# Two-part scores and a later cast in the attention stage of a fused GNN kernel

## The chip, the core and the metric
The kernel runs on one core of a Trainium2 chip. The time is the device time of one execution in microseconds. The kernel before takes 1899.82 us, the median of 3 runs (1897.61 to 1903.91).

## What is computed
The input is x (3125 nodes, 768 features, float32) and 50000 edges (src, dst) sorted by dst. Two layers with a layer norm, a relu and a residual each follow one another: a two-step graph convolution, and a graph attention with 12 heads of 64 features. The change touches only the attention:

```python
hh = h.reshape(n, H, D)
ft = einsum('nhd,ed->nhe', hh, W_fc)
a1 = einsum('nhd,hd->nh', ft, attn_l)
a2 = einsum('nhd,hd->nh', ft, attn_r)
e = leaky_relu(a1[src] + a2[dst], 0.2)
m = segment_max(e, dst)
ee = exp(e - m[dst])
denom = segment_sum(ee, dst)
agg = segment_sum((ee / denom[dst])[:, :, None] * ft[src], dst)
res = einsum('nhd,ed->nhe', hh, W_res)
x = x + relu((res + agg).reshape(n, H * D))
```

## The kernel before, in words
Destination nodes are cut into 25 tiles of 128 rows (the last has 53). A tile's edges are worked on in quads; with these inputs every tile has one quad, so there are 25 visits. A quad has four units, one for each 32 destination rows, of up to 512 edges each (4 chunks of 128), and one shared chunk for what is left over: 17 chunks. Each chunk is one indirect DMA of 128 rows from the table in HBM; a row holds, per head, 64 features and a one (780 numbers), and 12 score terms a1 behind them. The last visit has two units (9 chunks).

The engines run side by side, each with its own program, and meet at semaphores. `ring` has two halves, so a quad's rows are fetched while the quad before is computed.

- GpSimd (POOL, `fetch`, L1243): for quad q it waits until its slots (row numbers) are in, then asks for units 0, 1, 2, the shared chunk and unit 3 in this order. Before each unit it waits for `used[s]`: TensorE must have finished the products of quad q-2 out of the same part of the ring.
- VectorE (DVE): `carry`, then the maximum of the scores with their sloped copy (L1613), two scans for the segment maximum (L1616, L1619), the difference (L1621), the division for the tile before (L1567 to L1573), then it waits for the exponentials (`w_made`) and scales the rows of units 0, 1 and 2 by them (L1650, `scaled[s]`). Behind unit 2 it waits for all rows of the next quad to have landed and copies their terms (L1561, L1562, `take_terms`, `terms_in`). Then the shared chunk (L1657), the finish of tile j-2 (L1579) and the one-hots of quad q+2 (L1555).
- ScalarE (ACT, `follow`): casts the quad's one-hots to float32 (L1344, `cast_hot`, `hot_cast`), the exponentials for DVE (L1368, `w_made`) and for itself (L1372), a copy of the next quad's transposed one-hots (L1330), the tile's a2 (L1325), unit 3's rows scaled in 48 pieces (L1388), the sloped copy of the next scores (L1336, needs `z_sum` of TensorE), and `lay` for the tile before (L1354, 16 pieces).
- TensorE (PE, `visit`): transposes the differences (L1471, `t_made`) and the next one-hots (L1442), the residual product of tile j-2 (L1419), clears the accumulators (L1483), the products of units 0, 1 and 2 (L1492, each behind `scaled[s]`, all behind `hot_cast`), the next quad's scores (`scores(q + 1)`), the shared chunk's products (L1507) and unit 3's (L1492). `scores` has two kinds of terms, added in the same PSUM window: four matmul groups out of the one-hots, a2 and a constant (L1454 to L1457), and five that add the fetched terms (L1461), behind `terms_in`; the last sets `z_sum`.
- SyncE (SP): per visit one store of a finished tile (384 KB, L1277), one load of the turned activations (384 KB, L1268), the slots of quad q+2 (L1261) and four small loads (L1265). The two 384 KB transfers begin with the third visit.

By parity of q, TensorE's product code exists twice, and a branch picks one (`by_parity`).

Of the kernel before, what the change touches and what calls it, by code (L numbers as in the profile page):

```python
# [69 lines left out]
def gnn_kernel(nc, x, src, dst, w1t, b1, w2t, b2, wfc, wfct, attn_lt, attn_rt, wrest, out):  # L70
# [21 lines left out]
    with ctx:  # L92
# [984 lines left out]
        with ExitStack() as st:  # L1077
# [84 lines left out]
            def window(c0, n):  # L1162
                return ps_s[0:UH, W0 + c0:W0 + c0 + n]
# [7 lines left out]
            def is_last(j):  # L1171
                return isinstance(j, int) and j == NT - 1

            def units_of(j):
                return LU if isinstance(j, int) and j == NT - 1 else US


            def early_of(j):
                return min(3, units_of(j) - 1)
# [4 lines left out]
            def by_parity(eng, which, body):  # L1184
                with eng.If(which < 1):
                    body(0)
                with eng.Else():
                    body(1)
# [20 lines left out]
            def quad_bounds(eng):  # L1209
                return (eng.value_load(qptr[0:1, NT - 1:NT], min_val=1, max_val=QMAX), eng.value_load(qptr[0:1, NT:NT + 1], min_val=1, max_val=QMAX))  # L1210
# [9 lines left out]
            def tiles(eng, step):  # L1220
                for j in range(2):
                    step(j)
                with eng.Fori(2, NT - 1) as j:
                    step(j)
                step(NT - 1)

            def has_before(j, back=1):
                return not isinstance(j, int) or j >= back
            with nc.Block() as block:
# [87 lines left out]
                @block.scalar  # L1317
                def _(eng):
                    bounds = quad_bounds(eng)
                    eng.wait_ge(g_const, 2)  # L1320

                    def a2_of(j):
                        for s in range(US):
                            r = slice(s * UD, (s + 1) * UD)
                            last = eng.activation(a2_blk[r, s * H:(s + 1) * H], a2[r, ds(j, 1), :].rearrange("p a h -> p (a h)"), ACT.Copy)  # L1325
                        last.then_inc(a2_made, 1)

                    def turn_hot(q):
                        eng.wait_ge(hot_tr, q + 1)
                        eng.activation(hot_t[:, :, :].rearrange("p c e -> p (c e)"), ps_ht, ACT.Copy).then_inc(hot_tc, 1)  # L1330


                    def sloped(q):
                        eng.wait_ge(z_sum, q + 1)
                        eng.wait_ge(c_chain, q + 1)
                        eng.activation(top[:, 1:1 + WIN], window(0, WIN), ACT.Copy, scale=SLOPE).then_inc(z_low, 1)  # L1336

                    def cast_hot(q, j):
                        eng.wait_ge(hot_made, q + 1)
                        eng.wait_ge(used[units_of(j) - 1], q + 2)  # L1340
                        if units_of(j) < US:
                            eng.wait_ge(used[US - 1], bounds[0] + 2)
                        par = eng.snap(q % 2)
                        eng.activation(hot_f[:, :, :].rearrange("p c e -> p (c e)"), hot[:, ds(par, 1), :, :].rearrange("p a c e -> p (a c e)"), ACT.Copy).then_inc(hot_cast, 1)  # L1344


                    def lay(j):
                        eng.wait_ge(o_made, j + 1)
                        eng.sem_inc(passed, 1)
                        eng.wait_ge(o_fin, j + 1)  # L1350
                        for g in range(US):
                            for s in range(US):
                                c0 = g // 2 * 512 + g % 2 * GN
                                last = eng.activation(ps_n[s * UD:(s + 1) * UD, c0:c0 + GN], o[g * UD:(g + 1) * UD, s, :], ACT.Copy)  # L1354
                        last.then_inc(o_laid, 1)

                    def step(j):
                        mine = units_of(j) - 1

                        def follow(q, nth, left):  # L1360
                            cast_hot(q, j)
                            with eng.If(nth < 1):
                                eng.sem_inc(r_exp, 1)
                            with eng.Else():
                                eng.wait_ge(r_diff, q + 1)
                                eng.activation(ex[:, 1:2], ex[:, 0:1], ACT.Exp).then_inc(r_exp, 1)
                            eng.wait_ge(t_made, q + 1)
                            eng.activation(given_w, ps_e, ACT.Exp).then_inc(w_made, 1)  # L1368
                            if is_last(j):
                                eng.sem_inc(own_made, 1)  # L1370
                            else:
                                eng.activation(weight[:, :, :], ps_e[:, 0:CPU, mine * H:(mine + 1) * H], ACT.Exp).then_inc(own_made, 1)  # L1372
                            turn_hot(q + 1)
                            with eng.If(left < 2):
                                a2_of(j + 1)
                            with eng.Else():
                                eng.sem_inc(a2_made, 1)
                            if is_last(j):
                                with eng.If(nth < 1):
                                    lay(j - 1)  # L1380
                                sloped(q + 1)
                                return
                            eng.wait_ge(own_made, q + 1)
                            rows = ring[:, ds(eng.snap(eng.snap(q % 2) * RB + mine * CPU * FROW), CPU * FROW)]
                            for c in range(CPU):
                                for h in range(H):
                                    head = rows[:, c * FROW + h * FH:c * FROW + (h + 1) * FH]
                                    last = eng.activation(head, head, ACT.Copy, scale=weight[:, c, h:h + 1])  # L1388
                            last.then_inc(scaled[mine], 1)
                            sloped(q + 1)  # L1390
                            if has_before(j):
                                with eng.If(nth < 1):
                                    lay(j - 1)
                        tile_quads(eng, j, follow)
                    turn_hot(0)
                    a2_of(0)
                    sloped(0)
                    tiles(eng, step)

                @block.tensor  # L1400
                def _(eng):
# [42 lines left out]

                    def scores(q):
                        eng.wait_ge(hot_tc, q + 1)
                        eng.wait_ge(a2_made, q + 1)
                        if not isinstance(q, int):  # L1450
                            eng.wait_ge(w_made, q)
                            eng.wait_ge(own_made, q)
                        eng.sem_inc(passed, 1)
                        eng.matmul(window(0, P), a2_blk[:, :], hot_t[:, 0, :], start=True, stop=True, skip_group_check=True)  # L1454
                        eng.matmul(window(CPU * P, P), far[:, :].to_broadcast([P, UH]), ident[:, :], start=True, stop=True, skip_group_check=True)
                        eng.matmul(window(CPU * P, P), far_of[:, :], hot_t[:, CPU, :], start=False, stop=True, skip_group_check=True)
                        eng.matmul(window(P, CPU * P), a2_blk[:, :], hot_t[:, 1:UC, :].rearrange("p c e -> p (c e)"), start=False, stop=True, skip_group_check=True)  # L1457
                        eng.wait_ge(terms_in, q + 1)
                        eng.sem_inc(passed, 1)
                        for c in range(UC):  # L1460
                            last = eng.matmul(window(c * P, P), terms[:, c, :], ident[:, :], start=False, stop=True, skip_group_check=True)  # L1461
                        last.then_inc(z_sum, 1)

                    def step(j):
                        nu = units_of(j)

                        def visit(q, nth, left):
# [26 lines left out]
                                last.then_inc(used[s], 1)  # L1494

                            def first_products(b):
                                for s in range(early_of(j)):
                                    unit(b, s)

                            def other_products(b):  # L1500
# [10 lines left out]
                            eng.wait_ge(hot_cast, q + 1)  # L1511
                            eng.sem_inc(passed, 1)
                            by_parity(eng, eng.snap(q % 2), first_products)
                            scores(q + 1)
                            by_parity(eng, eng.snap(q % 2), other_products)
                        tile_quads(eng, j, visit)
                    turn_hot(0, 0)
                    scores(0)
                    tiles(eng, step)
                    natural(NT - 2)  # L1520

# [188 lines left out]
```

## Time and profile before

| what | value |
|---|---|
| median of 3 runs | 1899.82 us |
| profiled execution, its own time | 1901.22 us |
| its span | 1899.5 us |
| PE, DVE, ACT, POOL busy | 1327.0, 1123.7, 716.8, 1234.5 us |
| attention stage | from about 1300 us to the end |
| granted TensorE clock, mean | 0.881 |

The page shows shares over the whole span. The attention is the last third: from 1400 to 1800 us DVE is busy 84 to 86%, ACT 89 to 90%, POOL 75 to 76%, PE 64 to 70%, and the DMA engines 96 to 97%. None of these shares alone says what sets the pace; the stretch has to be read visit by visit, which recurs about every 22.3 us.

### The profile page before, as it was taken

Reading aid. Unit: us, or ns where it says so; the run is one execution under the profiler, and the core shown is the slowest. Engines: PE = TensorE matmul, PEld = TensorE weight load, DVE = VectorE, ACT = ScalarE, POOL = GpSimd, SP = SyncE. Lnnn points to the kernel's source line nnn. Section 1 sums busy time; section 2 is a strip of 40 time slices with the busy share of each in tenths; the row PEclk is TensorE's granted clock in tenths of the full one; section 3 lists DMA queues with packets and bytes.
Section 4 is the critical chain, followed back from the end, with each engine's and each line's share of the span. In section 5 each row is a group of like instructions: output and inputs, shape, how many; then the busy total and the mean of one; then the engine's idle time right before and its main releaser. Section 6 shows DMA issues by size and latency. Waiting matters only on the chain. (4 is left out here: it accounts for less than half of the span.)

```text
span 1899.5 us, 43588 instructions
## 1 busy us (share of the span) xinstructions
PE 1327.0 (70%) x13579; PEld 879.2 (46%) x13580; DVE 1123.7 (59%) x2027; ACT 716.8 (38%) x2184; POOL 1234.5 (65%) x1297
## 2 busy tenths in 40 slices
PE   6426877787877847777777777793566676677665
PEld 6314444444544524444444444492344544444453
DVE  6623454444544525545555555562788888888887
ACT  6600111111111100001000010171688998989885
POOL 3137777777777457777777777204777777777760
PEclk9977898989999978899999899997788878888887
DMA  6589999999999679999999999388999999999992
GB/s 219 208 210 361 331 328 336 333 332 331 335 334 330 230 239 334 330 324 329 323 333 334 330 326 331 140 322 291 314 335 347 348 352 347 345 347 343 357 320 69
DMA packets 139991, 585.22 MB, mean 308 GB/s; under 512 B 30615, under 2 KB 32751, under 8 KB 139945
## 3 DMA queue, kind: packets, MB, share of 16 engines
q0 software_dynamic: 100272, 497.49, 74.3%
q1 hardware_dynamic: 32563, 67.72, 10.1%
q10 hardware_dynamic: 7110, 19.43, 2.9%
q8 instruction: 25, 0.41, 0.1%
q14 instruction: 21, 0.17, 0.0%
HBM read 534.42 MB, written 50.12 MB: 308 GB/s over the span
## 5 line engine op out<-in xcount | busy, mean ns | idle before, releaser
L667 POOL DMA_INDIRECT ring_c<-table,slot_c x834 | 797.0, 956 | 313.6 <-issue 293.9
L1243 POOL DMA_INDIRECT ring<-table,slot x417 | 413.3, 991 | 141.5 <-issue 115.9
L711 ACT ACTIVATE slot_c<-units 128x8 int32 (+1 forms) x104 | 21.7, 210 | 857.9 <-DMA ring_c<-table,slot_c 812.0
L1388 ACT ACTIVATE ring<-ring,weight x1152 | 279.0, 335 | 0.6
L833 DVE TENSOR_TENSOR hots<-iota,units 128x256 f32<-128x256 bf16 x102 | 43.5, 428 | 391.3 <-PE ps_sum0a L779 123.0
L1650 DVE TENSOR_TENSOR ring<-ring,ps_w 128x3120 f32 x72 | 242.7, 3398 | 16.8 <-ACT ps_w L1368 16.5
L1492 PE MATMUL ps_acc<-ring,hot_f 128*32 128x195 f32 x3136 | 179.1, 376 | 86.0 <-DVE ring L1650 84.1
L808 PE MATMUL ps_ya<-weights,sum_ta 128*128 128x512 f32 (+1 forms) x576 | 190.9, 488 | 0.0
L808 PE MATMUL ps_yb<-weights,sum_tb 128*128 128x512 f32 (+1 forms) x576 | 189.7, 486 | 0.0
L1492 PEld LDWEIGHTS ps_acc<-ring,hot_f 128*32 128x32 f32 x3136 | 105.1, 124 | 148.1 <-DVE ring L1650 109.3
L808 PEld LDWEIGHTS ps_ya<-weights,sum_ta 128*128 128x128 f32 x576 | 110.2, 191 | 77.3 <-issue 69.6
L808 PEld LDWEIGHTS ps_yb<-weights,sum_tb 128*128 128x128 f32 x576 | 109.5, 190 | 76.4 <-issue 68.9
L779 PE MATMUL ps_sum0a<-ring_c,hots 128*32 128x192 f32 x1600 | 86.4, 368 | 78.5 <-DMA ring_c<-table,slot_c 78.5
L779 PE MATMUL ps_sum0b<-ring_c,hots 128*32 128x192 f32 x1600 | 84.9, 361 | 70.0 <-DMA ring_c<-table,slot_c 70.0
L779 PE MATMUL ps_sum1b<-ring_c,hots 128*32 128x192 f32 x1536 | 85.5, 373 | 64.2 <-DMA ring_c<-table,slot_c 64.2
L779 PE MATMUL ps_sum1a<-ring_c,hots 128*32 128x192 f32 x1536 | 85.7, 373 | 62.4 <-DMA ring_c<-table,slot_c 62.4
L1354 ACT ACTIVATE ps_n<-o_g 32x192 f32<-32x192 f32 x384 | 124.6, 324 | 7.7 <-DVE nodes L1579 3.6
L779 PEld LDWEIGHTS ps_sum0a<-ring_c,hots 128*32 128x32 f32 x1600 | 57.9, 121 | 104.8 <-issue 75.0
L779 PEld LDWEIGHTS ps_sum0b<-ring_c,hots 128*32 128x32 f32 x1600 | 57.5, 118 | 95.5 <-issue 79.9
L779 PEld LDWEIGHTS ps_sum1b<-ring_c,hots 128*32 128x32 f32 x1536 | 57.0, 122 | 90.5 <-issue 77.3
L779 PEld LDWEIGHTS ps_sum1a<-ring_c,hots 128*32 128x32 f32 x1536 | 56.9, 122 | 88.7 <-issue 79.2
L854 DVE TENSOR_TENSOR ps_sum0a<-ps_sum0a,naturala 32x192 f32<-32x192 f32 x200 | 73.3, 367 | 8.3 <-ACT naturala L739 5.7
(294 smaller groups left out, 1940.2 us busy)
## 6 DMA issues: line engine op xcount, KB each, us to landing
ring_c<-table,slot_c POOLq DMA_INDIRECT x834, 5.4
table<-ft SPq DMA_DIRECT2D x25, 396.0 KB, 2.8
table<-nodes SPq DMA_DIRECT2D x25, 384.0 KB, 3.3
table<-nodes ACTq DMA_DIRECT2D x25, 384.0 KB, 5.3
turned_table<-h_t SPq DMA_DIRECT2D x25, 384.0 KB, 3.0
nodes<-in_x ACTq DMA_DIRECT2D x24, 384.0 KB
turned_g<-turned_table SPq DMA_DIRECT2D x24, 384.0 KB, 6.5
out_x<-nodes SPq DMA_DIRECT2D x24, 384.0 KB
```

What stands on the lines that cost most here:

```text
L667: eng.indirect_dma_start(out=ring[:, t * QH + k, :], out_offset=None, in_=table, in_offset=bass.IndirectOffsetOnAxis(ap=slot[t][:, k:k + 1 ...
L711: eng.activation(slot[t][:, :], units[:, ds(q, 1), t * QH:(t + 1) * QH + t].rearrange("p a c -> p (a c)"), ACT.Copy).then_inc(slot_ready[t ...
L779: last = eng.matmul(block_of(par, s, g), hot, rows[:, g * GB:(g + 1) * GB], start=start, stop=True, skip_group_check=True)
L808: last = eng.matmul(product(jj)[:, c0:c0 + n], turned(jj)[:, k, :], w[:, k, c0:c0 + n], start=(k == 0), stop=(k == KB - 1))
L833: eng.tensor_tensor(hots[k][:, :, :].rearrange("p (s c) d -> p s c d", c=CPU), iota0[:, :].unsqueeze(1).unsqueeze(2).to_broadcast([P, 2, C ...
L854: last = eng.tensor_tensor(block_, block_, natural[s * UD:(s + 1) * UD, g * GB:(g + 1) * GB], ALU.add)
L1243: eng.indirect_dma_start(out=ring[:, b * RB + at * FROW:b * RB + (at + 1) * FROW], out_offset=None, in_=table3, in_offset=bass.IndirectOff ...
L1354: last = eng.activation(ps_n[s * UD:(s + 1) * UD, c0:c0 + GN], o[g * UD:(g + 1) * UD, s, :], ACT.Copy)
L1388: last = eng.activation(head, head, ACT.Copy, scale=weight[:, c, h:h + 1])
L1492: last = eng.matmul(acc_of(s, g), hot_f[:, c, s * UD:(s + 1) * UD], ring[:, x0 + g * GW:x0 + (g + 1) * GW], start=False, stop=True, skip_g ...
L1650: eng.tensor_tensor(mine, mine, given_w[:, 0:CPU, s * H:(s + 1) * H].unsqueeze(3).to_broadcast([P, CPU, H, FH]), ALU.mult).then_inc(scaled ...
```

## The change
In `follow` on ScalarE the cast of the one-hots is moved from the head of the visit to behind the two exponentials. On TensorE `scores` is split. Its first part (`scores_of_hots`, L1454 to L1457 with the waits for the one-hots, a2 and the exponentials of the quad) is issued behind unit 1's products, its second part (`scores_of_terms`, with the wait for `terms_in`) behind unit 2's. Unit 2's products get a parity branch of their own (`next_products`). The last tile has `early_of` 1 and no such branch. No arithmetic instruction is added or removed; the branch and one more increment of `passed` are.

```diff
 def follow(q, nth, left):
-    cast_hot(q, j)
     with eng.If(nth < 1):
         eng.sem_inc(r_exp, 1)
...
         eng.activation(weight[:, :, :], ps_e[:, 0:CPU, mine * H:(mine + 1) * H], ACT.Exp).then_inc(own_made, 1)
+    cast_hot(q, j)
     turn_hot(q + 1)
...
-def scores(q):
+def scores_of_hots(q):
     eng.wait_ge(hot_tc, q + 1)
     eng.wait_ge(a2_made, q + 1)
...
     eng.matmul(window(P, CPU * P), a2_blk[:, :], hot_t[:, 1:UC, :].rearrange("p c e -> p (c e)"), start=False, stop=True, skip_group_check=True)
+
+def scores_of_terms(q):
     eng.wait_ge(terms_in, q + 1)
     eng.sem_inc(passed, 1)
     for c in range(UC):
...
 def first_products(b):
-    for s in range(early_of(j)):
+    for s in range(min(2, early_of(j))):
+        unit(b, s)
+
+def next_products(b):
+    for s in range(2, early_of(j)):
         unit(b, s)
...
 by_parity(eng, eng.snap(q % 2), first_products)
-scores(q + 1)
+scores_of_hots(q + 1)
+if early_of(j) > 2:
+    by_parity(eng, eng.snap(q % 2), next_products)
+scores_of_terms(q + 1)
 by_parity(eng, eng.snap(q % 2), other_products)
```

## Rows read from the trace of the kernel before

**Rows 1.** The chain that ended last over the whole span, by engine.
```profile
issue 9%; POOL 5%; DVE 5%; ACT 4%; PE 3%; DMA 2%; DVEq 1%; ACTq 1%; SPq 0%; POOLq 0%
```

**Rows 2.** Busy time by windows: stretch, length, engines, PEclk, DMA share, GB/s.
```profile
1322.00:1343.60 21.60, 7.13 (x62) 4.89 (x66) 12.62 (x11) 10.50 (x35) 16.16 (x17) 0.50 0.93 319
1389.00:1835.00 446.00, 305.52 (x4040) 214.94 (x4040) 379.51 (x341) 398.03 (x1461) 338.02 (x341) 0.83 0.97 348
```

**Rows 3.** Timeline of one visit: start, length, engine, line, operation, idle before.
```profile
1564.81 6.71 DVE L1650 TENSOR_TENSOR ring<-ring,ps_w 128x3120 f32 x2
1568.26 1.75 PE L1492 MATMUL ps_acc<-ring,hot_f 128*32 128x195 f32 x32 [0.60 <-DVE ring L1650]
1571.58 1.53 PE L1492 MATMUL ps_acc<-ring,hot_f 128*32 128x195 f32 x32 [1.57 <-DVE ring L1650]
1572.25 0.22 DVE L1562 COPY terms<-ring 128x48 f32 x1
1573.72 1.02 PE L1457 MATMUL ps_s<-hot_t,a_blk 128*48 128x512 f32 x2
1574.58 1.26 PE L1461 MATMUL ps_s<-ident,terms 128*48 128x128 f32 x10
1575.88 0.70 ACT L1336 ACTIVATE top_g<-ps_s 48x640 f32<-48x640 f32 x1 [1.64 <-PE ps_s L1461]
1576.47 5.37 ACT L1354 ACTIVATE ps_n<-o_g 32x192 f32<-32x192 f32 x16
1580.73 0.82 DVE L1621 TENSOR_TENSOR score<-ps_s,top_g 48x640 f32<-48x640 f32 x1
1581.69 0.48 PE L1471 MATMUL ps_s<-ident,score 48*128 48x48 f32 x5 [3.07 <-DVE score L1621]
1582.27 0.74 ACT L1344 ACTIVATE hot_f<-hot 128x640 f32 x1 [0.43 <-issue]
1583.03 0.35 ACT L1368 ACTIVATE ps_w<-ps_s 128x240 f32<-128x240 f32 x1
1587.05 6.71 DVE L1650 TENSOR_TENSOR ring<-ring,ps_w 128x3120 f32 x2
```

**Rows 4.** Gathers on POOL, timeline; where a fetch starts, and a long one.
```profile
1367.36 0.94 POOL L1243 DMA_INDIRECT ring<-table,slot  x1 [2.58 <-PE ps_acc L1492]
1435.00 0.95 POOL L1243 DMA_INDIRECT ring<-table,slot  x1 [1.79 <-PE ps_acc L1492]
1457.00 0.95 POOL L1243 DMA_INDIRECT ring<-table,slot  x1 [0.30 <-issue]
1523.95 0.94 POOL L1243 DMA_INDIRECT ring<-table,slot  x1 [0.52 <-issue]
1568.51 0.94 POOL L1243 DMA_INDIRECT ring<-table,slot  x1 [0.52 <-issue]
1579.81 1.64 POOL L1243 DMA_INDIRECT ring<-table,slot  x1 [0.30 <-issue]
1590.48 0.95 POOL L1243 DMA_INDIRECT ring<-table,slot  x1 [0.30 <-issue]
1601.73 2.19 POOL L1243 DMA_INDIRECT ring<-table,slot  x1 [0.30 <-issue]
1835.38 0.95 POOL L1243 DMA_INDIRECT ring<-table,slot  x1 [0.30 <-issue]
```

**Rows 5.** The first visit's scores, timeline.
```profile
1350.75 1.06 PE L1457 MATMUL ps_s<-hot_t,a_blk 128*48 128x512 f32 x2 [2.06 <-issue]
```

**Rows 6.** The end of the stage, timeline.
```profile
1839.33 0.26 DVE L1561 COPY terms<-ring 128x192 f32 x1 [0.72 <-DMA ring<-table,slot]
1842.96 0.70 ACT L1336 ACTIVATE top_g<-ps_s 48x640 f32<-48x640 f32 x1 [1.64 <-PE ps_s L1461]
1860.89 1.53 PE L1492 MATMUL ps_acc<-ring,hot_f 128*32 128x195 f32 x32 [1.17 <-DVE ring L1650]
1865.19 0.70 ACT L1336 ACTIVATE top_g<-ps_s 48x640 f32<-48x640 f32 x1 [1.63 <-PE ps_s L1461]
```

More of the change, by code:

```diff
@@ L1517, in _ @@
                     turn_hot(0, 0)
-                    scores(0)
+                    scores_of_hots(0)
+                    scores_of_terms(0)
                     tiles(eng, step)
```

## The prediction, made before the changed kernel had run

> **What bounds the kernel now.** I read the whole-span chain of waits first, then windows over the attention stage, then one visit as a timeline, then every gather. The chain is mixed: no engine has more than a few per cent [rows 1]. So shares don't decide, and I look for loops. From 1389 to 1835 us twenty visits pass at 22.3 us each, with ACT busy 398 of 446 us, DVE 380, POOL 338, and the DMA engines at a share of 0.97 with 348 GB/s [rows 2].
>
> Loop A goes through DVE, PE and ACT, once a visit [rows 3]. DVE's third unit ends at 1564.81 + 6.71 = 1571.52. PE then does unit 2 (1571.58 + 1.53 = 1573.11), the one-hot groups (until 1573.72 + 1.02 = 1574.74) and the terms (until 1575.84). ACT's sloped copy ends at 1576.58. DVE's scans end with the difference at 1580.73 + 0.82 = 1581.55. PE's transposes end at 1582.17. ACT first does the cast (1582.27 to 1583.01), and only then the exponentials (1583.03 to 1583.38). DVE scales three units, until 1587.05 + 6.71 = 1593.76. From 1571.52 to 1593.76 are 22.24 us, and nothing in the loop waits for anything outside it. The terms were ready at 1572.47, 2.1 us before PE used them: the landing of rows is not on this loop now.
>
> Loop B is POOL: 17 gathers, each 0.945 + 0.303 us from start to start, make 21.22 us. One or two gathers of a fetch take longer (1579.81 lasts 1.64 us, 1601.73 lasts 2.19, [rows 4]); this comes about 5 us behind the two 384 KB transfers of a visit. Before these transfers exist the fetch from 1322 took 21.3 us at 319 GB/s [rows 2]. I take the excess for back-pressure of the DMA. It is 0.69 to 0.88 us in the fetches that began with a small wait (0.69 in the one gather of 1.64). Third, POOL waits for unit 0's products at a fetch's start: the gap is about 0.52 us in place of 0.30 in 13 fetches between 1411 and 1814 us, as at 1523.95 and 1568.51, once 1.79 (1435.00) and once 2.58 (1367.36) [rows 4]. 21.22 + 0.76 + 0.22 = 22.2: A and B are tied, with A ahead by the small wait.
>
> **The change part by part.** The cast. PE's transposes end at 1582.17 and ACT's `lay` at 1576.47 + 5.37 = 1581.84; the cast starts 0.43 us behind it. Without it the exponentials can start at about 1582.35 instead of 1583.03: 0.65 us less in loop A (bounds 0.5 and 0.74, the cast's own length). ACT's work from there on (copy of one-hots, a2, unit 3's rows) starts no later than now, as the total ahead of it is the same. `hot_cast` comes later by the two exponentials, at about 1583.7, but the first product that needs it starts when unit 0 is scaled, at 1587. Its waits for `used` and `hot_made` move behind the exponentials, which so lose them; both are met long before.
>
> The split. PE is idle from unit 1's end (1568.26 + 1.75 = 1570.01) to 1571.58. The one-hot groups take 1574.74 - 1573.11 = 1.6 us there, 0.3 us of control around them: unit 2 begins 0.1 to 0.5 us late. Then the terms follow unit 2 at once. From DVE's third unit to `z_sum` there are 4.32 us now; then 0.3 + 1.55 + 0.3 + 1.25 = 3.4. Gain 0.9 us (bounds: 0.3, if each of three new control steps costs 0.5; and 1.7, if all is hidden). All waits of the first part (transposed one-hots, a2, both exponentials) are met 7 us before. Behind it on PE's queue stand unit 2's products and POOL's unit 2 gathers, which need them only some 5 us later.
>
> Loop A falls to 22.24 - 0.65 - 0.9 = 20.7 us, so loop B sets the pace. What the time gains is what POOL stops waiting, and the ends of the stage, where POOL doesn't bind.
>
> Start: the wait of 2.58 - 0.30 = 2.28 us before the fetch at 1367.36 [rows 4]. It hangs on the scores of the second quad, which in the first visit ended late, behind a pause of 2.06 us inside the one-hot groups that nothing in the profile explains [rows 5]. The split brings these scores forward by 3.4 us if the pause falls in PE's idle time, by 1.1 if it moves to the terms; the cast was hidden there. I take 1.7 of 2.28 (bounds 0.5 and 2.28).
>
> The wait at 1435.00: 1.79 - 0.30 = 1.49 us, goes whole, since loop A is 1.5 us shorter in each of the visits before (bounds 1.0 and 1.49).
>
> The small waits: 13 of about 0.225, 2.9 us. Here the question is what the long gathers do. Five fetches began without a wait and without a large one just before; their excess was 0.97 to 1.25, as in the one that starts at 1590.48 and holds the 2.19 us gather [rows 4], against 0.75 behind a small wait: as if DMA took back what was given. But the fetch at 1435.00, without a wait behind it, had 0.75 as well. I take half, 1.5 us (bounds: the mean excess of the 20 fetches from 1389 us on is 0.84; at 1.25 in each 8.3 us are lost and 2.9 won back, 5.4 lost; at 0.75 in each 1.7 come on top of the 2.9, 4.6 won).
>
> End [rows 6]: the last full quad's rows are there at 1839.3 and its terms at 1839.8. PE finishes their scores at about 1842.93 now, and could at 1839.8 + 0.3 + 1.25 = 1841.4: 1.5. One exponential, 0.6. In the visit behind it DVE sets the pace: its third unit ends at 1860.84, the scores at 1865.15; 4.3 to 3.6 gives 0.7. The last visit's exponential comes 0.6 earlier by the cast. From there everything follows in the old order (the last visit has no part 2 branch). Sum 3.4 (bounds 2.2 and 4.0).
>
> Sum: 1.7 + 1.5 + 1.5 + 3.4 = 8.1 us. The profiled execution took 1901.2 (span 1899.5), so 1893.1 by its measure; it lies 1.4 above the median, which gives 1891.7 for the median, as 1892. Bounds: 0.5 + 1.0 - 5.4 + 2.2 = -1.7 and 2.3 + 1.5 + 4.6 + 4.0 = 12.4.
>
> On the DMA the rows show 348 GB/s as a mean at a share of 0.97 over twenty visits [rows 2], 7.75 MB a visit. The Trainium skill (DMA: Bandwidth & Descriptors, section Where 436 GB/s comes from) names about 358 GB/s as what HBM gives one core, and about 435 as what the ports carry. By the first a visit can't be under 21.6 us, which is below loop B; but so near to it that little can be won, and it speaks for the first rival. The same page says that single-core measurements reach 425.
>
> **The rivals.** First: DMA binds, and each removed wait comes back as a longer gather (fetches at 22.25 us, as the three between 1457.00 and 1523.95, the last followed by a small wait [rows 4]: 66.95 - 0.22 = 66.7). For it: DMA share 0.97, excess of 1.0 without waits. Against: the fetch at 1568.51 took 1590.48 - 1568.51 = 21.97. The 21 fetches from 1367.36 to 1835.38 took 468.0, at 22.25 they take 467.3; with 1.7 and 3.4 at the ends the gain is 5.8 us: 1894.
>
> Second: all waits go and the excess stays at 0.75. For it: 13 of 20 fetches show it. 2.3 + 1.5 + 4.6 + 4.0 = 12.4: 1887.
>
> Third: the split does nothing (the terms wait behind a late unit 2), and only the cast counts. Loop A then is 21.6 us, which still frees POOL: 0.2 + 1.5 + 1.5 + 3 x 0.6 = 5: 1895.
>
> Fourth, slower: PE pays a pause like the 2.06 us [rows 5] in each visit, at the new branch or behind it, on the way to the terms. Loop A is then 20.7 + 2.06 = 22.8 us and binds again: 20 x (22.8 - 22.3) = 10, and about 1 at the ends: 1911. It decides from a pause of 1.6 us on. For it: the pause exists, and the loop's code gets one more jump. Against: behind both present branches PE's steady visits show gaps of only 0.3 us. The Trainium skill (Runtime: NRT & Kernel Launch, section Instruction fetch mechanics) says that a taken branch out of the loaded window stalls for a fetch; the present branches over longer code show no such stall in steady visits.
>
> **How the numbers follow.** A measurement of this kernel can tell about 0.3%, 5.7 us, from no change: faster is below 1894.1, slower above 1905.5. The forecast has 0.50, of which a good four fifths lie below 1894.1; DMA binds 0.20, somewhat under half of it below; all waits go 0.13; only the cast 0.10, a third of it below; slower 0.07. Faster: 0.42 + 0.09 + 0.13 + 0.04 = 0.68; same 0.25; slower 0.07. The range from 1886 to 1899 takes in the first three rivals and most of the bounds.
>
> **What would show it.** The exponential starts within 0.3 us of the transposes' end. One-hot groups stand between units 1 and 2, and the terms start within 0.5 us of unit 2 or of the terms' copy. DVE's wait for landed rows grows from 0.6 to 1.1 to about 2 us a visit. POOL's gaps at a fetch's start are all 0.30 us; the excess of the long gathers is 0.75 to 1.0 a fetch (1.0 and more: first rival). Fetches follow every 22.0 to 22.2 us. The prediction is wrong if the visits get shorter than 21.9 us (the excess was no back-pressure), if PE pauses by over 1.6 us ahead of the terms, or if the stage's end keeps its length.

## The result, and the profile after

The changed kernel takes 1890.35 us (median of 8 runs, 1886.72 to 1893.94), the kernel before 1903.43 beside it on the same chip (8 runs, 1897.61 to 1904.87). The ratio is 0.994, with a 95% interval from 0.9926 to 0.9955: 8.6 to 14.1 us less, 11.4 by the ratio itself (the two medians lie 13.1 apart). The profiled execution took 1886.80 us with a span of 1885.0.

Where it went, by the starts of fetches (a fetch is the 17 gathers of one quad) in the two traces. The columns are the start of the stage's first gather, the time from it to the start of the 4th fetch, the 21 fetches from there, and the rest, in us:

```
kernel   first gather  to 4th fetch  21 fetches   to the end  stage total
before      1300.76        66.60       468.02       64.12        598.7
after       1295.28        65.45       462.65       61.62        589.7
```

"Stage total" is the span less the first gather's start. Of the 14.5 us between the two spans 5.5 lie ahead of the stage, where the code is the same; over nine profiled executions on this kind of chip, the kernels of the experiments below among them, the first gather starts anywhere from 1295.2 to 1301.3. So 9.0 us are the change's: 1.15 at the start, 5.37 in the middle, 2.50 at the end. Each kernel has one trace; how much the stage itself varies between executions is not known.

The middle of the stage, one window of the kernel after, with the columns of [rows 2]:

```profile
1389.00:1823.00 434.00, 292.21 (x3962) 208.76 (x3958) 374.43 (x336) 391.96 (x1433) 332.04 (x335) 0.85 0.97 352
```

One visit of the kernel after as a timeline, as in [rows 3]:

```profile
1555.60 6.71 DVE L1660 TENSOR_TENSOR ring<-ring,ps_w 128x3120 f32 x2
1561.20 1.02 PE L1457 MATMUL ps_s<-hot_t,a_blk 128*48 128x512 f32 x2
1562.23 0.25 DVE L1571 COPY terms<-ring 128x192 f32 x1
1562.37 1.53 PE L1494 MATMUL ps_acc<-ring,hot_f 128*32 128x195 f32 x32
1563.82 1.29 PE L1463 MATMUL ps_s<-ident,terms 128*48 128x128 f32 x10
1565.71 0.69 ACT L1336 ACTIVATE top_g<-ps_s 48x640 f32<-48x640 f32 x1
1571.51 0.48 PE L1473 MATMUL ps_s<-ident,score 48*128 48x48 f32 x5 [3.61 <-DVE score L1631]
1572.31 0.35 ACT L1367 ACTIVATE ps_w<-ps_s 128x240 f32<-128x240 f32 x1 [0.65 <-PE ps_s L1473]
1572.80 0.74 ACT L1344 ACTIVATE hot_f<-hot 128x640 f32 x1
1576.33 6.71 DVE L1660 TENSOR_TENSOR ring<-ring,ps_w 128x3120 f32 x2
1584.61 0.49 DVE L1571 COPY terms<-ring 128x192 f32 x1 [1.57 <-DMA ring<-table,slot]
1585.33 1.26 PE L1463 MATMUL ps_s<-ident,terms 128*48 128x128 f32 x10 [0.72 <-DVE terms L1572]
1588.11 0.70 ACT L1336 ACTIVATE top_g<-ps_s 48x640 f32<-48x640 f32 x1 [1.57 <-DVEq L1617]
```

The one-hots' groups stand ahead of unit 2, and the terms follow it at once. The exponentials start 0.32 us behind the transposes' end (1571.99), the cast behind them. DVE's third unit ended at 1555.60 + 6.71 = 1562.31 and ends again at 1576.33 + 6.71 = 1583.04: loop A is 20.73 us in this visit, where it was 22.24. The last three rows show what is late next: DVE waits 1.57 us for landed rows, and then ACT's sloped copy waits 1.57 us for DVE.

The waits of the middle (1380 to 1830 us) by who waited for what (us in total, times, longest). DVEq is DVE's sequencer:

```profile
DVE terms L1571 <- DMA ring<-table,slot: 26.8, 20, 1.8
ACT top_g L1336 <- DVEq L1617: 22.9, 18, 1.7
POOL ring L1243 <- PE ps_acc L1494: 6.7, 22, 0.3
```

And the fetches' first gathers on POOL, with the end of the stage's last full quads:

```profile
1360.73 0.94 POOL L1243 DMA_INDIRECT ring<-table,slot  x1 [1.32 <-PE ps_acc L1494]
1382.36 0.95 POOL L1243 DMA_INDIRECT ring<-table,slot  x1 [0.30 <-issue]
1823.38 0.95 POOL L1243 DMA_INDIRECT ring<-table,slot  x1 [0.30 <-issue]
1827.18 0.26 DVE L1571 COPY terms<-ring 128x192 f32 x1 [1.10 <-DMA ring<-table,slot]
1830.59 0.70 ACT L1336 ACTIVATE top_g<-ps_s 48x640 f32<-48x640 f32 x1 [1.01 <-DVEq L1617]
1837.20 0.35 ACT L1367 ACTIVATE ps_w<-ps_s 128x240 f32<-128x240 f32 x1 [0.65 <-PE ps_s L1473]
1857.66 0.35 ACT L1367 ACTIVATE ps_w<-ps_s 128x240 f32<-128x240 f32 x1 [0.38 <-PE ps_s L1473]
```

The 2.58 and 1.79 of [rows 4] are 1.32 and 0.30 now, and the small waits are 0.30 to 0.33 but for one of 0.48: 21 fetches take 462.65 us, 22.03 each.

### The profile page after: what moved, and what is told of

Its sections match the earlier page's. It is cut to its first block and busy times, and to the rows that moved or that the text cites. A ratio compares the mean times of both kernels' runs of the same rounds, so it can differ in the third digit from the quotient of the medians.

```text
span 1885.0 us, 43624 instructions
## 1 busy us (share of the span) xinstructions
PE 1328.8 (70%) x13579; PEld 879.1 (47%) x13580; DVE 1124.0 (60%) x2027; ACT 716.7 (38%) x2184; POOL 1230.6 (65%) x1297
## 5 line engine op out<-in xcount | busy, mean ns | idle before, releaser
L1494 PE MATMUL ps_acc<-ring,hot_f 128*32 128x195 f32 x3136 | 163.4, 352 | 50.9 <-DVE ring L1660 44.6
L1494 PEld LDWEIGHTS ps_acc<-ring,hot_f 128*32 128x32 f32 x3136 | 99.9, 117 | 114.5 <-DVE ring L1660 80.8
L779 PE MATMUL ps_sum1a<-ring_c,hots 128*32 128x192 f32 x1536 | 81.9, 364 | 57.7 <-DMA ring_c<-table,slot_c 57.6
L1473 PE MATMUL ps_s<-ident,score 48*128 48x48 f32 x125 | 16.7, 282 | 109.9 <-DVE score L1631 109.9
```

The costliest lines, as they stand in the source:

```text
L779: last = eng.matmul(block_of(par, s, g), hot, rows[:, g * GB:(g + 1) * GB], start=start, stop=True, skip_group_check=True)
L1494: last = eng.matmul(acc_of(s, g), hot_f[:, c, s * UD:(s + 1) * UD], ring[:, x0 + g * GW:x0 + (g + 1) * GW], start=False, stop=True, skip_g ...
```

## The experiments

### The parts one by one, and another order on SP

"Cast only" is the part of the change in ACT's list, "split only" that in PE's. "Early load" is the kernel after with SP's two large transfers in the other order:

```diff
-                            store(j - 2)
+                            eng.wait_ge(o_nat, j - 1)
+                            eng.sem_inc(passed, 1)
                             load_turned(j - 1)
+                            store(j - 2)
```

They ran first on another chip, beside the change itself.

> The changed kernel once more, beside the parts of it. My theory (the pace passed from the loop through DVE, PE and ACT to POOL's gathers): ratio 0.994 to 0.996, fetches every 22.0 to 22.2 us, sum of the attention stage from the first gather to the end 9 us shorter than before (589.7 against 598.7 us). The 5.5 us by which the first gather came earlier in the first profile of the changed kernel (1295.3 against 1300.8 us) are spread between executions and not the change: here the first gather may lie anywhere from 1294 to 1302. If the change also shortened the part ahead of the stage (by where its code lies), the first gather is again at 1295 to 1296.

> Only the cast is moved; the scores stay in one part behind unit 2. Theory: the loop through DVE, PE and ACT falls from 22.24 to about 21.6 us, already under POOL's pace of 22.0 to 22.2, so most of the gain in the middle comes from this part alone: 5 to 6 of the 9 us, ratio about 0.997; POOL's small waits are gone, and a landing wait of 1.3 us appears ahead of the terms. Rival (the split carries the gain, as the cast is 0.65 of 1.5 us): ratio 0.999 and POOL still waits at a fetch's start.

> Only the scores are split; the cast stays ahead of the exponentials. Theory: the loop falls from 22.24 to about 21.3 us, which is also under POOL's pace: 6 to 7 of the 9 us, ratio about 0.9965. So the two parts overlap: their gains together are more than the whole. Rival (each part acts by itself): the gains of the two parts add up to that of the whole.

> The changed kernel, but SyncE loads the turned activations of the next tile (384 KB) as soon as TensorE has read the last ones, about 11 us earlier than now, and not directly behind the 384 KB store. Theory (a long gather is back-pressure behind the two transfers coming together): the excess of 0.85 us a fetch falls to 0.2 to 0.5, fetches come every 21.5 to 21.8 us, and the time falls by 6 to 12 us against the changed kernel. Rival one (DMA binds as a whole, 348 GB/s is all there is): fetches stay at 22.1 us, the excess only moves to another gather. Rival two (the long gathers come from the scans on DVE, with which they coincide): the excess stays at the same gather.

Measured against the kernel before (2290.71 us there): the change 0.9974 [0.9959, 0.9989], cast only 0.9999 [0.9985, 1.0012], split only 0.9977 [0.9964, 0.9991], early load 0.997 [0.9956, 0.9984]. This chip is 20% slower, and something else bounds the kernel there, which these runs don't name. A window of the change there:

```profile
1700.00:2200.00 500.00, 356.31 (x3593) 215.22 (x3591) 335.80 (x301) 355.13 (x1298) 301.06 (x300) 0.81 0.83 273
```

273 GB/s in place of 352, fetches 28.4 us apart, PE's products in small groups with idle time "issue" between them (89.3 us of these 500), and gathers that wait for something the profile calls remote (62.7 us of these 500). So these four say how the change does where transfers are slow, 0.3% in place of 0.6% and by the split alone, and little on loops A and B. The forecasts for the change (0.994 to 0.996), the cast (0.997) and the early load (6 to 12 us below the change) missed here. I repeated them on a chip like the first:

> Only the cast is moved. The same question as in the run of the cast alone before, whose chip moved 272 GB/s and needed 28.4 us a fetch with or without the change, so that it could not tell. Where DMA gives 345 GB/s again: the loop through DVE, PE and ACT falls from 22.24 to 21.6 us, below POOL's 22.0 to 22.2; by theory 5 to 6 of the 9 us come from this part alone, ratio 0.997. By the rival, in which the split carries it, ratio 0.999.

> Only the scores are split. Theory: the loop falls to 21.3 us, 6 to 7 of the 9 us, ratio 0.9965; with the cast alone it overlaps, the two gains add up to more than the whole. Rival (each acts by itself): they add up to 0.994 to 0.9955, the ratio of both. On a chip with 272 GB/s: ratio 0.9975 as before.

> The changed kernel with the load of the turned activations right behind their last use. Theory (a long gather is back-pressure behind two 384 KB transfers that come together): excess down from 0.85 to 0.2 to 0.5 us a fetch, fetches every 21.5 to 21.8 us, ratio 0.989 to 0.992 to the kernel before. Rival one (DMA binds as a whole): fetches stay at 22.1 us, ratio 0.994 to 0.996 as of the changed kernel, the excess sits at another gather. Rival two (scans on DVE make the long gathers): excess and place unchanged.

Cast only: 0.9978 [0.9967, 0.999], 4.2 us less than 1901.52. Split only: 0.9971 [0.9957, 0.9986], 5.5 us less. Together 9.7, and the change 11.4 [8.6 to 14.1]: each part alone is worth about half, and the sum can't be told from the whole. That the two gains add up to more than the whole, as I expected, is not shown by the times. In the traces their stages are 596.1 and 590.9 us, and the 21 fetches take 464.4 us with either, 3.6 less than before, where both give 5.4. Each leaves one of the waits: the first row is of cast only, the second fence of split only.

```profile
1363.60 0.94 POOL L1243 DMA_INDIRECT ring<-table,slot  x1 [3.83 <-PE ps_acc L1492]
```
```profile
1451.29 0.94 POOL L1243 DMA_INDIRECT ring<-table,slot  x1 [1.76 <-PE ps_acc L1494]
```

The head's wait stays without the split, and is longer: the pause of [rows 5] stands in the same place there, 2.83 us long. The wait of the middle (1.79 in [rows 4]) comes back in another visit without the cast.

Early load: 0.9985 [0.9974, 0.9995], only 2.9 us less than before, so some 8 us worse than the change, where I had expected 15 to 21 us less than before. Its fetches 4 to 24 take 471.4 us. The trace:

```profile
1648.58 0.36 SPq L1268 DMA_DIRECT2D turned_g<-turned_table  x1
1658.31 0.28 DVE L1573 COPY terms<-ring 128x192 f32 x1 [3.05 <-DMA ring<-table,slot]
1676.04 0.95 POOL L1243 DMA_INDIRECT ring<-table,slot  x1 [2.44 <-PE ps_acc L1496]
```

The load stands among the fetch's last gathers now. DVE waits 3.05 us for their rows (34.6 us in 17 visits, 26.8 in 20 after the change), and POOL then waits 2.44 for the products. That the load delays these rows is my reading; no run separates it. The excess of the long gathers, which back-pressure should have moved with the load, was 0.61 us a fetch and stayed with DVE's work: all 27 long gathers (over 1.03 us) of the 21 fetches begin in the two DVE operations named below, at places 6 to 12 of a fetch.

### Is the excess back-pressure of the transfers?

The kernel after without the visit's load (the residual product reads the first tile's activations each time), and with 16 columns stored of each row instead of all, so that its result is incomplete: 0.78 MB less per visit.

```diff
-  eng.dma_start(whole[:, ds(jj, 1), :], nodes[:, ds(jj, 1), :]).then_inc(out_st, 16)
+  eng.dma_start(whole[:, ds(jj, 1), 0:16], nodes[:, ds(jj, 1), 0:16]).then_inc(out_st, 16)
...
-                            load_turned(j - 1)
+                            eng.sem_inc(passed, 1)
```

> The changed kernel, in which SyncE does not load the turned activations of a tile (the residual product reads the first tile's each time) and stores only 16 of 768 columns of each full tile of the attention's result: about 0.78 MB a visit less. Theory (the excess is back-pressure behind these transfers; POOL's own pace is 21.22 us): fetches every 21.3 to 21.4 us as in the two fetches before the first store, some 15 us less than the changed kernel, ratio 0.986. If the excess has another cause (scans, slots), fetches stay at 22.1 us. If the loop through DVE, PE and ACT is longer than my 20.7 us, it binds above 21.4.

0.9936 [0.9913, 0.9959], as the change, where back-pressure called for 0.986. Its window has a DMA share of 0.93 and 316 GB/s, and the excess is 0.86 us a fetch, at the same gathers. The first row is its window, the second fence one long gather with DVE's work beside it:

```profile
1389.00:1831.00 442.00, 295.88 (x4044) 211.31 (x4040) 380.91 (x341) 398.49 (x1461) 337.93 (x340) 0.86 0.93 316
```
```profile
1599.06 1.54 DVE L1629 TENSOR_TENSOR_SCAN top_g<-same_g,top_g 48x640 f32<-48x640 bf16 x1
1599.27 2.09 POOL L1243 DMA_INDIRECT ring<-table,slot  x1 [0.30 <-issue]
```

Back-pressure falls. The second fence shows what stands there instead: the gather starts 0.21 us into DVE's backward scan, whose two inputs both lie in SBUF, and ends at 1601.36, 0.76 us after the scan's end (1600.60). The trace of before had it all along, in the very gathers of [rows 4]; its scans:

```profile
1579.15 1.54 DVE L1619 TENSOR_TENSOR_SCAN top_g<-same_g,top_g 48x640 f32<-48x640 bf16 x1
1601.61 1.54 DVE L1619 TENSOR_TENSOR_SCAN top_g<-same_g,top_g 48x640 f32<-48x640 bf16 x1
```

They end at 1580.69 and 1603.15; the gathers of 1.64 and 2.19 us end at 1581.45 and 1603.92, 0.76 and 0.77 later. So the length says only how early in the scan the gather came. The operations are two: this scan, and the one-hots of 0.81 us (L1555 before, L1565 after). All 34 long gathers in the stage of the trace before, and all 36 after, start in one of them, 0.06 us in or later, and end 0.75 to 0.77 us after the scan or 0.81 to 0.83 after the one-hots. The other way round, of the gathers that start 0.10 us in or later, every one that these ends would make at least 1.03 us long was (34 before, 35 after); two that started 0.07 and 0.09 us into a scan were not held. The forward scan, nearly as long (1.48 us) but with one input in PSUM, is the control: 17 gathers start in it before that such an end would lengthen, and all last 0.94 or 0.95 us. Two SBUF inputs may not be the only way to hold one: once in each trace a gather starts 0.05 us into the terms' copy (0.26 us, one SBUF input) and ends 0.81 to 0.82 after it, 1.02 or 1.03 us long.

### The operation's input moved to PSUM

The kernel after with the one-hots' iota, the ramp that they are compared with, in PSUM (A), with the backward scan reading PSUM in two pieces (B), and both. A also turns the iota from bfloat16 to float32 (the operation takes 0.81 us as before), and B's forward scan writes to PSUM in two pieces. The core of A and of B:

```diff
+            iota_p = ps_l[:, 76:76 + UD]
-  eng.tensor_tensor(hot[...], iota0[:, :].unsqueeze(1)...
+  eng.tensor_tensor(hot[...], iota_p.unsqueeze(1)...
...
-  eng.tensor_tensor_scan(top[:, 0:WIN][:, back], same[:, 1:1 + WIN][:, back], top[:, 0:WIN][:, back], top[:, WIN:1 + WIN], ...)
+  eng.tensor_tensor_scan(top[:, WA:WIN][:, back], same[:, WA + 1:1 + WIN][:, back], fwd_b[:, 0:WIN - WA][:, back], fwd_b[:, WIN - WA:1 + WIN - WA], ...)
+  eng.tensor_tensor_scan(top[:, 0:WA][:, back], same[:, 1:1 + WA][:, back], fwd_a[:, back], top[:, WA:WA + 1], ...)
```

> The changed kernel with one input of the one-hots' comparison on DVE (L1565) in PSUM (the ramp as float32) and not in SBUF. New theory: a gather on POOL is held while DVE runs an operation whose two inputs both lie in SBUF, the backward scan (L1629) or the one-hots (L1565), if the operation is running 0.18 us after the gather's start; the gather then ends 0.76 us after it. Then the long gather at place 5 of a fetch is gone, that at place 9 stays (0.3 to 1.2 us): excess about 0.9 to 1.0 without those of 0.3 to 0.6 at place 5, fetches every 21.9 to 22.1 us, 0 to 4 us less than the changed kernel. Old theory (back-pressure of DMA): places 5 and 9 as before.

> The changed kernel with the forward scan written to PSUM, in two pieces of 400 and 241 columns, and the backward scan, also in two pieces, reading it there, so that no scan has two inputs in SBUF. New theory: the long gather at place 9 is gone, only the one-hots' at place 5 is left (0.1 to 0.6 us in some fetches): excess 0.2 to 0.4 a fetch, fetches every 21.5 to 21.7 us unless the loop through DVE, PE and ACT binds, which the pieces lengthen from 20.7 to about 21.3 us: 8 to 12 us less than the changed kernel, ratio 0.988 to 0.991. Old theory: place 9 as before, and the time no better or 1 us worse. If the loop has grown by over 1 us (pieces dearer than 0.2 us each), POOL waits at a fetch's start and the gain is lost.

> Both: no DVE operation of the attention loop has two large inputs in SBUF. New theory: no gather is longer than 1.0 us but for the terms' copies, fetches every 21.3 to 21.5 us, or the DVE loop's own length if that is more; ratio 0.986 to 0.990. Old theory: fetches at 22.1 us.

Against before (1900.98 us): A 0.9954 [0.9939, 0.9969], B 0.9932 [0.9909, 0.9955], both 0.9926 [0.9903, 0.995]. The gathers from 1362 to 1827 us, grouped (count, busy us, mean ns, idle before), one fence each for after, A, B and both:

```profile
L1243 POOL DMA_INDIRECT ring<-table,slot x359 | 355.6, 990 | 109.6 <-issue 101.0 <-PE ps_acc L1494 7.0 <-DMA slot<-unit_table 1.2
```
```profile
L1244 POOL DMA_INDIRECT ring<-table,slot x357 | 354.3, 992 | 111.4 <-issue 97.2 <-PE ps_acc L1495 10.5 <-DMA slot<-unit_table 3.0
```
```profile
L1246 POOL DMA_INDIRECT ring<-table,slot x364 | 347.4, 954 | 118.9 <-issue 101.6 <-PE ps_acc L1497 13.6 <-DMA slot<-unit_table 2.4
```
```profile
L1247 POOL DMA_INDIRECT ring<-table,slot x363 | 343.2, 945 | 122.7 <-issue 101.3 <-PE ps_acc L1498 19.3 <-DMA slot<-unit_table 1.2
```

In the 21 fetches no gather of 357 is longer than 1.03 us with both (32 after, 20 with A, 8 with B). It is not that they miss the operations now: in the whole stage of "both" 14 gathers start in the pieces of the backward scan and 5 in the one-hots so that the ends above would have lengthened them, and all last 0.94 or 0.95 us; with A alone it is 13 in the one-hots, and none is held. One of them with both, which by its start 0.22 us into a piece would have taken 1.58:

```profile
1399.56 1.04 DVE L1639 TENSOR_TENSOR_SCAN top_g<-same_g,top_g,ps_l 48x400 f32<-48x400 bf16 x1
1399.78 0.94 POOL L1247 DMA_INDIRECT ring<-table,slot  x1 [0.30 <-issue]
```

With A all 20 long ones start in the scan, and they are longer (0.84 us of excess each, 0.53 for the 20 in the scan after), so the excess stays at 0.83 us a fetch: what one hold gives back, the other takes. The cause of the long gathers is shown: one input moved to PSUM ends the hold, in each operation by itself. What it brings is small, and less than I expected (0.986 to 0.990 for both). Both together save 0.78 us a fetch and gain 4.8 of the 16 us over 21 fetches (462.65 to 457.84), 3.6 over the stage; B alone takes 457.41. POOL's waits for PE grow from 7.0 to 19.3 us in the rows above, and one visit of both shows where:

```profile
1587.74 0.26 DVE L1576 COPY terms<-ring 128x192 f32 x1 [1.25 <-DMA ring<-table,slot]
1602.32 2.54 PE L1498 MATMUL ps_acc<-ring,hot_f 128*32 128x195 f32 x32 [0.15 <-DVE ring L1670]
1605.71 0.94 POOL L1247 DMA_INDIRECT ring<-table,slot  x1 [1.87 <-PE ps_acc L1498]
```

The fetch from 1561.63 has its rows landed at 1587.74 (26.1 us), unit 0's products of them end at 1604.86 (17.1), and the fetch that reuses the buffers starts at 1605.71: 44.1 us for two visits. A third loop, from landed rows through DVE, ACT and PE to the buffers' reuse, over two fetches, binds in some visits. Timed, B and both lie below the change (0.9932 and 0.9926 beside 0.994), but the intervals overlap: not told apart.

### How much slack loop A has

The kernel after with the difference (L1631) made twice, 0.82 us and a gap more in loop A by its row:

```diff
+                            for k in range(1):
+                                eng.tensor_tensor(score[:, :], window(0, WIN), top[:, 1:1 + WIN], ALU.subtract).then_inc(z_max, 1)
+                                eng.wait_ge(z_max, q * 2 + k + 2)
```

> The changed kernel with the difference on DVE (L1631, 0.82 us) done twice in each visit, the second behind a wait for the first: 0.85 to 0.9 us more in the loop through DVE, PE and ACT, and in the way from landed rows to unit 0's products. Theory: the loop alone takes 20.7 us of a pace of 22.0, and the chain of fetch, landing (26.3 us), scores and unit 0 (16.0), and POOL's start (0.85) takes 43.2 of 44.1 us that two fetches take; 0.9 us just fit into both. So the time grows by 0 to 4 us, ratio to the kernel before 0.994 to 0.997, with small waits of up to 0.3 us at the starts of fetches, and with DVE's wait for landed rows down from 1.3 to about 0.5 us a visit. Rival (the loop still sets the pace, and the change gained by something else): 21 visits times 0.87, 18 us more than the changed kernel, ratio 1.003 to 1.005.

0.9986 [0.9972, 1.0] against 2313.26 us: it ran on a slow chip again, where fetches are 28 to 29 us apart and loop A can't show its slack. On the chip of the result the slack of loop A stays open.

## Why the prediction was right, and where it was not

It said 1892 us, 8.1 less, and 1890.35 was measured, 11.4 less with 8.6 as the lower end. The direction is right, and so is the main mechanism: loop A falls below loop B, and the time gains what POOL stops waiting and the two ends. The gain was taken too small. That the time itself is off by only 1.7 us is in part luck: the 1899.82 it was taken from, a median of 3 runs, lies 3.6 below the 1903.43 of the kernel before beside the result. In the stage 9.0 us went where 8.1 were forecast, and there too errors cancel: the start (1.15 for 1.7) and the end (2.50 for 3.4) were taken too large, the middle (5.37 for 3.0) too small.

The cast: forecast 0.65 us off loop A, measured 0.54: from the transposes' end to the exponentials there were 1583.03 - 1582.17 = 0.86 us, and there are 1572.31 - 1571.99 = 0.32. The split: 0.9 forecast; from the third unit's end to the sloped copy there are 1565.71 - 1562.31 = 3.40 us now and 4.36 before, so 0.96. Loop A was forecast at 20.7 and is 20.73. The fourth rival is refuted: from 1380 to 1830 us no idle time of PE that is put down to "issue" is longer than 0.5 us. One pause like that of [rows 5] is there, ahead of that stretch, in the second visit, within unit 3's products:

```profile
1371.12 1.19 PE L1494 MATMUL ps_acc<-ring,hot_f 128*32 128x195 f32 x21 [2.19 <-issue]
```

It costs nothing that shows, as the transposes behind it still wait 1.25 us for DVE. DVE waits 1.34 us a visit for landed rows (26.8 in 20), where about 2 were forecast.

Head: 1.7 us of the wait were to go, 1.26 went (2.58 to 1.32), though the pause of [rows 5] is gone from the scores of the second quad and its best case said 2.28. The wait of 1.49 went whole.

Small waits and excess: I took half of 2.9 us, as the excess might grow back. The middle gained 5.37 where 1.5 + 1.5 were forecast. The small waits themselves gave 4.2 (4.44 us over 21 fetches, 0.25 now, the large one of 1.49 within), and the excess, 0.86 us a fetch before, is 0.81. This is the term that was mis-sized, and it is so because **its cause was wrong**: I read the excess as back-pressure of the DMA from where it stood, behind the two large transfers. It was a hold between DVE and POOL, whose length depends on where in DVE's operation a gather starts, not on what the DMA has to move. The sign that I had set for it, visits shorter than 21.9 us, didn't show this (22.03). The fetch of 1.25, which I took for time taken back, held a gather that started 0.12 us into the scan. The middle ran nearly as in the second rival (5.37 for its 6.1); the head and the end kept the sum below its 12.4.

End: forecast 3.4 us, measured 2.50. The exponentials of its first two visits before:

```profile
1850.11 0.35 ACT L1368 ACTIVATE ps_w<-ps_s 128x240 f32<-128x240 f32 x1
1872.08 0.35 ACT L1368 ACTIVATE ps_w<-ps_s 128x240 f32<-128x240 f32 x1
```

In the visit that DVE paces the gain was 1.5 (exponential to exponential 20.46 us, 21.97 before), against 0.7 + 0.6. In the visit behind the landing it was 0.76 against 2.1: from the terms' copy to the exponential 10.02 us, 10.78 before. This term was mis-sized too. The step that failed is that ACT's sloped copy follows PE's scores. PE is early as forecast, but the copy also waits for DVE's carry, which stands behind DVE's shared chunk, the finish of tile j-2 and the one-hots (the wait for L1617, 22.9 us in 18 visits above, 1.01 in this one). I had moved one of two inputs.

The first rival is out: the fetches take 22.03 us and not 22.25, 352 GB/s are moved, and with both inputs in PSUM the fetches take 21.80, with the gathers at 945 ns. With both, the window from 1389 to 1823 us moves 355 GB/s at the same share: the 0.97 was no limit to 352.

On this hold the Trainium skill (SBUF — State Buffer, section Who interferes with whom) says that a DVE instruction with two SBUF inputs contends with a GpSimd instruction that reads SBUF, and infers that a DMA issued from GpSimd isn't stalled by such a `tensor_tensor`, since making descriptors needs only the write side. The first half agrees with the traces, the second does not: indirect gathers, whose indices lie in SBUF, were held by a `tensor_tensor` of 0.81 us and a scan of 1.54, and freed by a PSUM input. The page's section A bandwidth-pool intuition that's wrong gives "DVE-end + ~115 ns" as the end of a blocked transfer; here it is 0.75 to 0.77 us behind the scan and 0.81 to 0.83 behind the one-hots.

## What to carry to other kernels

Before a long instruction is put down to the transfers near it, set its end against the ends of what other engines did beside it: a constant distance from an operation's end points at the cause, a mere place in the loop doesn't, and an edit of that operation alone settles it. When an edit brings an operand forward, list every operand of the next instruction; the gain is that of the last one. Where two loops are nearly tied, shortening one gives the small waits between them; shortening the second may meet a third loop, here after 0.23 us a visit.

## What the hardware showed unexpectedly

A POOL gather of 0.945 us lasts up to 2.19 when it starts in a DVE operation with two SBUF inputs, and keeps its length when one of them lies in PSUM. Chips differ: the kernel before takes 1901 to 1903 us on some and 2291 to 2313 on others, where a window of the attention stage moved 273 and 267 GB/s. The same code ahead of the stage varied by 6 us between profiled executions, as much as half of this change.
